# Second cross attention of a four-layer kernel: seven slots of two key tiles a unit, or four phases of three or four key tiles

## What is computed

```python
scale = DIM_HEAD ** (-0.5)
qn = layernorm(x, ln_q_g, ln_q_b)
q = qn @ Wq * scale
kv = media @ Wkv
k, v = jnp.split(kv, 2, axis=-1)
...
sim = jnp.einsum('bhid,bhjd->bhij', q, k)
sim = jnp.where(media_mask[:, None, None, :], sim, neg_inf)
attn = jax.nn.softmax(sim, axis=-1)
out = jnp.einsum('bhij,bhjd->bhid', attn, v)
```

## Time and profile before

| | |
|---|---|
| median of three executions | 3631.37 us |
| span of the profiled execution | 3628.6 us (its page gives no other time; the median is 2.8 us above it) |
| PE busy | 3390.8 us, 93% |
| DVE busy | 2019.1 us, 56% |
| ACT busy | 1846.1 us, 51% |
| POOL busy | 1589.9 us, 44% |
| the stage of the change | about 1626 to 3044 us of the span |

### The profile page before, as it was taken

One profiled execution on the slowest core, in us unless ns is written; L12 is line 12 of the kernel. 1 busy time (PEld: TensorE's weight loads), 2 busy tenths in 40 slices (PEclk: granted clock), 3 DMA queues, 4 the chain that ended last, 5 costly groups with the idle time before them and its releaser, 6 DMA issues. The chain is left out here.

```text
span 3628.6 us, 74082 instructions
## 1 busy us (share of the span) xinstructions
PE 3390.8 (93%) x25048; PEld 2305.3 (64%) x25048; DVE 2019.1 (56%) x3324; ACT 1846.1 (51%) x3374; POOL 1589.9 (44%) x1421
## 2 busy tenths in 40 slices
PE   7798799898999799989999999999999998999997
PEld 5556544344444388866666666666666666878886
DVE  4465577776777454435555555555555553114454
ACT  2254277676776533335555555555555553333333
POOL 3213012221221011107777777777777775005554
PEclk9899799999999899999999999999999999999998
DMA  4784200000000222220000000000001003220200
GB/s 120 170 131 120 79 7 18 17 17 17 17 18 27 96 74 100 107 112 10 13 31 14 32 13 32 16 30 15 33 29 42 13 13 119 82 75 1 98 7 12
DMA packets 74751, 179.36 MB, mean 49 GB/s; under 512 B 14720, under 2 KB 44928, under 8 KB 68480
## 3 DMA queue, kind: packets, MB, share of 16 engines
q1 hardware_dynamic: 70240, 161.81, 14.7%
q0 software_dynamic: 4128, 12.60, 1.3%
HBM read 115.09 MB, written 59.26 MB: 48 GB/s over the span
## 5 line engine op out<-in xcount | busy, mean ns | idle before, releaser
L1654 POOL TENSOR_TENSOR cross_acc<-cross_acc,cross_probs 128x512 f32<-128x512 f32 (+1 forms) x704 | 921.4, 1309 | 159.9 <-ACT cross_probs L1717 118.6
L1717 ACT ACTIVATE cross_probs<-cross_s,cross_bias 128x512 f32<-128x512 f32 (+1 forms) x832 | 530.3, 685 | 488.9 <-PE cross_s L1936 487.1
L1813 DVE TENSOR_REDUCE cross_partmax<-cross_r 128x1 f32<-128x400 f32 (+1 forms) x1024 | 541.2, 570 | 334.3 <-PE cross_r L1906 316.0
L1256 DVE TENSOR_REDUCE cross_partmax<-cross_m 128x2 f32<-128x800 f32 (+1 forms) x512 | 497.0, 991 | 187.1 <-PE cross_m L1359 186.1
L1167 ACT ACTIVATE cross_probs<-cross_s 128x512 f32<-128x512 f32 (+1 forms) x832 | 453.9, 596 | 150.7 <-PE cross_s L1379 150.4
L1949 PE MATMUL cross_av<-cross_probs,cross_v 128*64 128x256 f32 (+1 forms) x3328 | 459.1, 394 | 0.0
L1949 PEld LDWEIGHTS cross_av<-cross_probs,cross_v 128*64 128x64 f32 (+1 forms) x3328 | 199.5, 136 | 173.2 <-ACT cross_probs L1717 77.3
L1106 POOL TENSOR_TENSOR cross_diag<-c_ident,cross_negmax 128x256 fp32r<-128x256 f32 x128 | 76.0, 615 | 497.6 <-DVE cross_negmax L1264 497.6
L1390 PE MATMUL cross_av<-cross_probs,cross_v 128*32 128x256 f32 (+1 forms) x3328 | 269.0, 395 | 10.2 <-ACT cross_probs L1167 9.0
L1802 DVE TENSOR_TENSOR cross_k_lo<-cross_r,cross_k_hi 128x400 fp32r<-128x400 f32 (+1 forms) x256 | 146.4, 572 | 192.4 <-ACT cross_k_hi L1695 192.4
L1930 PE MATMUL cross_s<-cross_q_hi,cross_k_hi 64*128 64x256 f32 (+1 forms) x1664 | 253.0, 299 | 0.0
(11 more groups left out here) (307 smaller groups left out, 6479.6 us busy)
## 6 DMA issues: line engine op xcount, KB each, us to landing
d_masked_ctx<-tail_ctx_split SPq DMA_DIRECT2D x8, 1602.0 KB, 5.3
d_self_qk<-selfproj_qk_split POOLq DMA_DIRECT2D x32, 256.0 KB, 5.5
self_qs<-d_self_qk SPq DMA_DIRECT2D x64, 128.0 KB, 8.0
self_ks<-d_self_qk SPq DMA_DIRECT2D x64, 128.0 KB, 8.5
d_cross<-tail_pr SPq DMA_DIRECT2D x8, 1024.0 KB, 4.6
cross_qp<-d_cross SPq DMA_DIRECT2D x64, 128.0 KB, 2.4
d_cross<-cross_out SPq DMA_DIRECT2D x64, 128.0 KB, 1.8
tail_attn<-d_cross SPq DMA_DIRECT2D x8, 1024.0 KB, 5.5
```

Of the source, the lines that this page charges most:

```text
L1256: nc.vector.tensor_reduce(partmax[:, :, jt // 2, jt % 2, i:i + 1], m_pair(sets[q], w), AX.X, ALU.max).then_inc(maxed, 1)
L1654: nc.gpsimd.tensor_tensor(acc[0:w, g % 2], left, probs[0:w, slot % NPB], ALU.add).then_inc(added, 1)
L1717: nc.scalar.activation(probs[0:w, (g * KT + t) % NPB], src_, ACT.Exp, scale=XHD ** -0.5, bias=bias[0:w, p, t:t + 1]).then_inc(probs_ready, 1)
L1813: nc.vector.tensor_reduce(partmax[:, m, i:i + 1], r_ps[MAX_BANK[q]][:, 0:KCH[i][1]], AX.X, ALU.max).then_inc(maxed, 1)
```

## The change

A unit has four **phases** in place of seven slots. The 13 tiles are divided into groups of 4, 3, 3 and 3 (`GROUPS`), each scored in two sets (`SETS`, now eight). Phase k of unit u holds, on PE: two maxima of unit u+1, the first score set, two maxima, the second score set, key chunk k of unit u+2, a value tile if there is one for this k, in phase 3 the shift of unit u+1, and the value products of group k-1 (in phase 0: of group 3 of the unit before, and then that unit's sums). The banks are the same in every phase: key chunk in 1, value tile in 2, shift and sums in 0, maxima in 0, 1, 2, 0. ACT and DVE follow the same order. No matmul, copy, reduction or transfer is added or taken away inside a unit.

```diff
-        SETS = [range(t, min(t + 2, KT)) for t in range(0, KT, 2)]
-        NS = len(SETS)
-
-        K_BANK, V_BANK, SHIFT_BANK, SUM_BANK = (2, 1, 0, 2), (0, 2, 0, 1), 1, 1
-        MAX_BANK = (0, 1, 2, 0, 2, 0, 1, 2, 1, 2, 0, 1, 0, 1, 2, 0)
...
+        SETS = [range(lo, hi) for lo, hi in ((0, 2), (2, 4), (4, 6), (6, 7), (7, 9), (9, 10), (10, 12), (12, 13))]
+        GROUPS = [range(0, 4), range(4, 7), range(7, 10), range(10, 13)]
+        NS, NQ = len(SETS), len(GROUPS)
+
+        K_BANK, V_BANK, SHIFT_BANK, SUM_BANK = (1, 1, 1, 1), 2, 0, 0
+        MAX_BANK = (0, 1, 2, 0) * 4
...
+                def phase(u, nxt, k, before):
                     after = nxt and following(nxt, NP)
...
+                    for s in (2 * k, 2 * k + 1):
+                        for t in SETS[s]:
+                            exponential(u, s, t)
+                    if after:
+                        k_high(after, k)
+                    made = value_tile(u, k)
+                    if made:
+                        v_tile(*made, r_ps[V_BANK])
+                    if before:
+                        copy_av(before)
+                        inverse_sum(before)
...
+                    for k in range(NQ):
+                        for q in range(4 * k, 4 * k + 4):
+                            maxima(nxt, q)
+                        if k == NQ - 1:
+                            diagonals(nxt)
+                        if after:
+                            k_low(after, k)
                     copy_shift(nxt)
...
+                def max_item(u, nxt, q, before):
+
+                    n, after, k = nxt[3], following(nxt, NP), q // 4
+                    if q == 0:
+                        pe.wait_ge(shifted, n + PRIME)
+                        pe.wait_ge(k_ready, (n + 1) * NC + PRIME)
+                    elif q == 2 and before and value_tile(before, NQ - 1):
+                        pe.wait_ge(v_ready, value_made(before, NQ - 1) + PRIME)
+                    elif q == 4:
+                        pe.wait_ge(ln_ready, n - 1 + PRIME)
+                        pe.wait_ge(maxed, n * NM + 4 + PRIME)
+                    elif q % 4 == 1 and k and after:
+                        pe.wait_ge(k_ready, (n + 1) * NC + k + PRIME)
+                    elif q % 4 == 2 and k and value_tile(u, k - 1):
+                        pe.wait_ge(v_ready, value_made(u, k - 1) + PRIME)
+                    elif q > 2:
+                        pe.wait_ge(maxed, n * NM + (q, q - 3, q - 3, q - 2)[q % 4] + PRIME)
+                    maxima(nxt, q)
+
+                def phase(u, nxt, k, before):
                     after = nxt and following(nxt, NP)
...
+                    if nxt:
+                        max_item(u, nxt, 4 * k, before)
+                        max_item(u, nxt, 4 * k + 1, before)
+                    scores(u, 2 * k)
+                    if nxt:
+                        max_item(u, nxt, 4 * k + 2, before)
+                        max_item(u, nxt, 4 * k + 3, before)
+                    scores(u, 2 * k + 1)
+                    if after:
+                        pe.wait_ge(maxed, nxt[3] * NM + 4 * k + 2 + PRIME)
+                        k_chunk(after, k)
+                    made = value_tile(u, k)
+                    if made:
+                        pe.wait_ge(maxed, nxt[3] * NM + 4 * k + 3 + PRIME)
+                        v_tile(*made, r_ps[V_BANK])
+                    if nxt and k == NQ - 1:
+                        shift(nxt)
+                    if k:
+                        values(u, k - 1)
+                    elif before:
+                        values(before, NQ - 1)
                         if nxt:
...
+                            pe.wait_ge(maxed, nxt[3] * NM + 4 + PRIME)
                         sums(before)
```

More of the change, by code:

```diff
@@ L1736, in ahead @@
                     for i in range(NC):
[L1737 removed]
+                        k_high(u, i, K_BANK_AHEAD)
                     for t in range(KT):
                         v_tile((0, 0, 0), t, ahead_bank(t))
[L1740 to L1764 removed]
@@ L1766, in step @@
-                def step(u, nxt):
-                    for s in range(1, NS):
-                        slot(u, nxt, s)
-                    if nxt:
-                        slot(nxt, following(nxt, NP), 0)
-                    inverse_sum(u)
+                    for i in range(NC):
+                        k_high(second, i, K_BANK_AHEAD)
+                def phase(u, nxt, k, before):
+                    after = nxt and following(nxt, NP)
+                    for s in (2 * k, 2 * k + 1):
[9 more added lines that the diff above has]
+                        inverse_sum(before)
@@ L1773, in start, with step @@
+                def step(u, nxt):
+                    for k in range(1, NQ):
+                        phase(u, nxt, k, None)
+                    if nxt:
+                        phase(nxt, following(nxt, NP), 0, u)
+                    else:
+                        copy_av(u)
+                        inverse_sum(u)
                 def start(u):
                     ahead(u)
-                    slot(u, following(u, NP), 0)
+                    phase(u, following(u, NP), 0, None)
                 units(act, NP, start, step)
@@ L1835, in ahead @@
                     for i in range(NC):
-                        k_low(u, i)
+                        k_low(u, i, K_BANK_AHEAD)
                     for q in range(NM):
-                        maxima(u, q)
+                        maxima(u, q, MAX_BANK_AHEAD)
                     diagonals(u)
                     copy_shift(u)
-                    for i in range(3):
-                        k_low(second, i)
                     queries(second)
-                    k_low(second, 3)
+                    for i in range(NC):
+                        k_low(second, i, K_BANK_AHEAD)
                 def step(u, nxt):
@@ L1977, in ahead @@
                     pe.wait_ge(maxed, 15 + PRIME)
-                    k_chunk(second, 0)
+                    k_chunk(second, 0, K_BANK_AHEAD)
+                    k_chunk(second, 1, K_BANK_AHEAD)
                     pe.wait_ge(maxed, NM + PRIME)
@@ L2032, in slot, with value_made @@
[L2032 to L2055 removed]
+                def value_made(u, j):
+                    (b, p, h), t = value_tile(u, j)
+                    return (b * 2 + h) * KT + t + 1
@@ L2056, in slot @@
                         if nxt:
-                            pe.wait_ge(maxed, nxt[3] * NM + 2 + PRIME)
+                            pe.wait_ge(maxed, nxt[3] * NM + 4 + PRIME)
                         sums(before)
                 def step(u, nxt):
-                    for s in range(1, NS):
-                        slot(u, nxt, s, None)
+                    for k in range(1, NQ):
+                        phase(u, nxt, k, None)
                     if nxt:
-                        slot(nxt, following(nxt, NP), 0, u)
+                        phase(nxt, following(nxt, NP), 0, u)
@@ L2069, in start @@
                     ahead(u)
-                    slot(u, following(u, NP), 0, None)
+                    phase(u, following(u, NP), 0, None)
                 units(pe, NP, start, step)
```

154 lines of the change are left out of this document (30 added, 124 removed).

## The result

The changed kernel is slower: **3690.3 us** median (3687.7 to 3699.9, 4 runs) against 3634.7 (3630.8 to 3647.6) for the kernel before beside it, a ratio of 1.0151 with the interval 1.0127 to 1.0175. That is 55.6 us more, where the prediction had 38 more (3669, range 3640 to 3712). The profiled execution took 3699.85, the slowest of the four, with a span of 3698.1. Of its 69.5 us over the span before, only part lies in the stage of the change.

The account below looks back on a forecast made before the run. PE's own stream was taken to bound the kernel at 22.16 us a unit; 1.73 saved against two new waits totalling 2.33 gave 0.60 more, +37 over 62 units, about 1 at the ends: 3669 us, range 3640 to 3712.

Parts of the forecast that it names:

- The base: Stage of the change before it: PE's own stream sets the time, busy 1390 of 1400 us, 22.16 us a unit.
- The price of a change of shape: On PE, each switch between matmul tile shapes costs about 0.2 us; the change takes them from 20 to 12 a unit.
- the 1.7 us that the change saves: PE's phases added up without waits: 20.43 us a unit, 1.73 less than 22.16, of which 1.6 from fewer shape changes.
- The shift's wait: Phase 3: PE stands at the shift until DVE has the diagonals, at 4.45 us of the phase; 1.66 us on average.
- The sums' wait: First maximum of phase 1 waits for ACT's logarithm to free the sums' bank; 0.67 us a unit, 0.40 at the lower bound.
- The unit's length: Four phases of 6.52, 5.17, 4.85 and 6.22 us on PE: 22.76 us a unit, 0.60 more than before.
- All four units: Sign in the changed kernel's trace: units of 22.8 us from negated maximum to negated maximum, all four alike.
- rival 3: Slower still: late exponentials hold second maxima of phases 2 and 3, 0.6 to 0.9 us a unit, 3706 to 3725; chance 0.17.
- bank chain: Bank 1: exponentials, `k_high`, `k_low` must finish before the next phase's second maximum; PE may go on at 4.74 us, costed at nothing.
- a rule behind it: Skill's clock-gate rule: the clock falls only after longer idle stretches than this stage's, so the clock's cost is nothing.
- Rival 1: Changes of shape decide: the saved drains on PE make it faster, 20.43 us a unit, 107 us less, 3524; chance 0.10.
- What I cost at nothing: Work taken as covered: bank 1, value tiles, POOL's additions, loads and stores, DVE's shift copy under the products of 1.44 us.

## Why the prediction was right, and where it was short

The time, 3690.3, is 21 us over the likeliest case and inside its range; 3.3 of the 21 are the base, since the kernel before has a median of 3634.7 beside this result and not 3631.4.

**The base was right.** PE set the time before: doubling a DVE instruction there changed nothing. No run changed PE's own stream in that kernel; in the order with the maxima earlier, where PE hardly waits, six more changes of shape lengthened every unit.

**The price of a change of shape was right**, 0.24 measured against 0.2 from the rows, and nearly so the 1.7 us that the change saves. With the sums in bank 2, phases 0 to 2 hold no wait and last 5.78, 5.29 and 4.88 us, against 5.74, 5.28 and 4.85 in the sum; phase 3 reaches the shift's place at 2.63, against 2.62. So the phases without waits were some 0.1 short, and the saving is about 1.6.

**The shift's wait was right in cause, 0.15 too long in size.** It went with the diagonals made a phase sooner, and grew when they were made twice. The shift came at 4.31 of the phase instead of 4.45. The chain on DVE ended 0.06 later than in the sum (4.25 against 4.18), and the way from DVE to PE, put at 0.27 from the value tile's row, is 0.06 here. Phase 3 was 6.19 against 6.22, since the shift and the products behind it, 1.88, took 0.11 more than their terms.

**The sums' wait was right in cause, 0.2 too dear.** From the sums to the next maximum 1.09 were measured against 1.31: ACT's logarithm ended at 1912.04 and PE went on at 1912.10, so the way from ACT to PE is 0.06, near the lower bound that I had named and not taken. The maxima and scores behind the wait then run a little longer, 5.38 for phase 1 against 5.17, which gives the 0.2 back: the first pair of maxima takes 0.29, so entering the shape was not hidden by the wait, as I had it. Both phases together are 0.65 longer than with the sums in bank 2, where I had 0.67.

**The unit's length is partly luck.** The four phases are 6.34, 5.38, 4.88 and 6.19 us, in sum 22.79 against 22.76. Two pairs of errors cancel in it: the two in the sums' wait, and the shift's wait, 0.15 too long, against the phases and the products behind the shift, together 0.2 too short.

**All four units are not alike.** I had forecast that. Once in four units the value tile of phase 0 is the first of a new half of a batch. ACT's copy of it (`v_tile`) then waits until the last products that read the old half are done, and the new order puts these products into phase 0 too. ACT stands there 14 times, 15.2 us in all (`cross_v` for `cross_av` in the view above); the kernel before has no such wait. The logarithm comes later by it, and PE's wait ahead of phase 1 is 0.81 or more instead of 0.48; that unit is 23.05 to 23.3, a quarter to half a microsecond over the others. This term was missed; over some 15 such units it is 4 to 7 us. It is the same copy for which the sums wait in the kernels with the sums in bank 2.

**The step that fell short is the clock.** The prediction took the stage at the full granted clock and kept the clock in rival 3, as a bound of 28 us beside the bank chain, and with a rule behind it by which it would be nothing. Measured: 11 falls, 17 us, in a kernel without any bank chain. The Trainium skill, TensorE: Matmul & The Clock Gate, Why this matters for your kernels, warns only of idle stretches longer than these. The Trainium skill reports there as well, under A second HAM failure mode, a kernel whose clock swings with short and frequent ones. The trace does not bear out the rule as the prediction used it: the clock fell to 0.50 behind 10 of the 37 waits for the diagonals that left PE idle for 1.5 us, and beside 38 of 53 waits in the kernel with the diagonals twice. That the wait brings the falls is shown: they went when it was removed or filled, stayed when the sums' wait was removed, and multiplied when it was lengthened. What picks the ten stays open.

The stage grew by 53.7 us from its first to its last negated maximum. 17 of them are the clock, and 37 are left, as many as the forecast had for the two waits less the saving. The fourth units are in these 37; against them, the edges are 0.1 to 0.4 us shorter than before, and the units of the last two batches, which stand behind the loop, grew by 0.4 instead of 0.6 to 0.7. The medians differ by 55.6, the spans of the two profiled executions by 69.5, with the 14.8 ahead of the stage.

**Rival 1 was priced too low in time.** Its 3524 took 20.43 us a unit as soon as the waits go. With both waits gone in this order the unit is 21.33 to 22.4 and the time 3605: ACT's and DVE's work at the turn of the unit binds next. In "What I cost at nothing" DVE's copy of the shift lies under the products; that held with phase 3 at 6.2 us, and it did not hold for a phase 3 of 4.39, which the rival took for granted. It touches the rival's price, not the forecast. The order that moves the maxima too came to 3566.

**Rival 3's bank chain did not come**: one wait of 0.8 us for `k_lo` in the stage, though the cover forecast in phase 2 was only 0.1 plus the first maximum.

## What to carry to other kernels

Grouping work by shape on the matmul engine has a price list that the trace gives, here 0.2 us a change; but each step that is put closer to its producer must be checked against that producer's whole chain, here four maxima, a reduction and the diagonals on DVE. Here moving the producer's part one phase ahead made the grouping pay: 3566 us instead of 3690. And count a wait on the matmul engine as possibly more than its length: here the clock fell behind 10 of 37 waits of 1.5 us in a stage that was busy otherwise. Check last which buffer each moved step frees: the products, one phase later, held up a copy on ACT that no one had waited for.

## What the runs showed of the hardware

- The granted clock fell from 2.4 to 1.2 GHz for some 3.4 us behind 10 of 37 single waits of 1.5 us, in a stage in which PE was busy 91%; each fall cost 1.55 us. Matmuls whose result nobody read, in the gap, kept it up.
- A wait of 3.2 us at the same place cost 62 by 1.6 us in length and about as much again by the clock: 38 of 53 such waits had a fall beside them, most of which began inside the wait and lasted about 6.8 us.
- A change of shape cost PE 0.24 us, measured by adding six to a unit, and 0.2 read from the distances of starts.
- From the end of a DVE or ACT instruction to the start of the matmul that waits for it 0.06 us passed. In the kernel before, 0.27 had been worked out for a value tile's wait for DVE.
- The same 128x512 multiply on DVE took 1.34 us, and 1.75 us right behind another one of its kind.
- The unit at an edge of the loop lasts some 3 us more than the others in the changed kernel (26.1), some 4 more in the kernel before (26.45 and 26.13 against 22), and 7 to 9 us more in every kernel with the sums in bank 2. The cause was not found.
